# Cross-attention: row sums carried over the blocks on VectorE, and the keys' high half written by ScalarE

## What is computed

```python
def _L0_xattn_ref(hidden_states, audio_tokens, attention_mask, Wq, bq, Wk, bk, ...):
    q = proj(hs, Wq, bq, S)          # 16 heads of 32, 256 queries
    k = proj(at, Wk, bk, T)          # 4096 keys
    v = proj(at, Wv, bv, T)
    scores = einsum('bhsd,bhtd->bhst', q, k) / scale
    scores = clip(where(attend, scores, -10000.0), -50.0, 50.0)
    probs = softmax(scores, axis=-1)
    ctx = einsum('bhst,bhtd->bhsd', probs, v)
    delta = ctx @ Wo.T + bo          # then a layer norm
```

## Time and profile before

| | before |
|---|---|
| median of 3 runs | 757.49 us (756.22 to 758.24) |
| the profiled execution | 755.26 us |
| its span, first to last instruction | 753.4 us |
| PE busy | 726.6 us (96%) |
| DVE busy | 600.6 us (80%) |
| ACT busy | 413.7 us (55%) |
| PE clock granted | 1.0 of full speed over the whole span |
| the pairs of blocks 0 to 6 | 37.5 to about 301 us |
| the last block, and the rest of the cross-attention | to about 336 us |

### The profile page before, as it was taken

How to read it: one execution, slowest core, us unless ns; L and a number is a source line. 1 busy time by engine, 2 the same in 40 slices (tenths; PEclk the granted TensorE clock), 3 DMA queues, 4 the chain that set the end, 5 groups by cost and what they waited for, 6 DMA issues and landing times.

```text
span 753.4 us, 16700 instructions
## 1 busy us (share of the span) xinstructions
PE 726.6 (96%) x6859; PEld 451.1 (60%) x6859; DVE 600.6 (80%) x948; ACT 413.7 (55%) x553; POOL 10.3 (1%) x30
## 2 busy tenths in 40 slices
PE   7999999999999999898799988999999999999997
PEld 3544444444444444445677756677777777777774
DVE  4588888888888888678888975788888888888885
ACT  3567676767676767733577753444444444444441
POOL 2000000000000000001000000000000000000000
PEclk9999999999999999999999999999999999999999
DMA  8910101010100010004124320396777777777760
GB/s 318 333 61 1 58 2 58 1 58 2 58 2 2 2 58 2 2 14 200 43 105 147 135 92 1 111 291 231 232 237 239 236 231 235 232 235 242 238 209 29
DMA packets 29576, 93.79 MB, mean 124 GB/s; under 512 B 5920, under 2 KB 15056, under 8 KB 28112
## 3 DMA queue, kind: packets, MB, share of 16 engines
q1 hardware_dynamic: 29232, 92.97, 37.6%
q10 hardware_dynamic: 288, 0.02, 0.0%
HBM read 92.37 MB, written 0.57 MB: 123 GB/s over the span
## 4 chain that ended last, share of the span: by engine, by line
PE 85%; DVE 6%; issue 4%; ACT 3%; POOL 1%; POOLq 0%; DVEq 0%; ACTq 0%
PE pS L1113 38%; PE pP L1113 26%; PE pO L1113 10%; PE pD L1113 9%; DVE xT L806 2%; ACT arena L485 2%; PE pO L1441 1%; DVE arena L691 0%; DVE bn L842 0%; DVE arena L821 0%; DVE arena L941 0%; DVE arena L893 0%; DVE xn L685 0%; ACT arena L535 0%; DVE work L847 0%
## 5 line engine op out<-in xcount | busy, mean ns | idle before, releaser
L1113 PE MATMUL pS<-arena 128*128 128x256 f16 (+2 forms) x2128 | 251.5, 274 | 5.1 <-DVE arena L941 1.3
L1113 PEld LDWEIGHTS pS<-arena 128*128 128x128 f16 (+2 forms) x2128 | 210.9, 101 | 49.5 <-ACT arena L552 2.2
L1113 PE MATMUL pP<-arena 128*128 128x512 f16 x968 | 235.2, 381 | 3.2 <-DVE arena L691 3.2
L1113 PEld LDWEIGHTS pP<-arena 128*128 128x128 f16 x968 | 90.7, 98 | 127.5 <-issue 22.0
L485 ACT ACTIVATE arena<-pS,mblk 128x1024 f32<-128x1024 f32 x128 | 147.3, 1201 | 14.2 <-PE pS L1113 11.5
L941 DVE SCALAR_TENSOR_TENSOR arena<-arena 128x1536 f16<-128x1536 f32 x72 | 126.0, 1751 | 0.1
L794 DVE TENSOR_SCALAR arena<-arena 128x1024 f32<-128x1024 f32 x128 | 88.3, 692 | 45.0 <-ACT arena L485 41.8
L628 ACT ACTIVATE arena<-pS 128x256 f32<-128x256 f32 x72 | 27.6, 384 | 156.6 <-PE pS L1113 156.6
L590 ACT ACTIVATE arena<-arena 128x1536 f16<-128x1536 f32 x72 | 106.3, 1477 | 0.3 <-DMA arena<-in_units 0.3
L1113 PE MATMUL pO<-arena 128*32 128x256 f32 (+6 forms) x1358 | 103.4, 358 | 2.4 <-DVE arena L931 1.9
L1113 PE MATMUL pD<-arena 128*128 128x512 f16 x288 | 76.5, 379 | 1.0 <-DVE arena L1085 1.0
(11 more groups left out here) (232 smaller groups left out, 499.4 us busy)
## 6 DMA issues: line engine op xcount, KB each, us to landing
arena<-in_units SPq DMA_DIRECT2D x72, 768.0 KB, 4.9
arena<-w_scratch SPq DMA_DIRECT2D x136, 64.0 KB, 2.7
arena<-in_ctxT SPq DMA_DIRECT2D x7, 1024.0 KB, 5.0
mw_in<-in_mla_in SPq DMA_DIRECT2D x8, 832.0 KB, 6.0
mw_out<-in_mla_out SPq DMA_DIRECT2D x8, 512.0 KB, 3.6
wlatT<-in_wlatT SPq DMA_DIRECT2D x1, 1280.0 KB, 11.9
arena<-in_wkT SPq DMA_DIRECT2D x4, 256.0 KB, 4.7
arena<-in_ctxT SPq DMA_DIRECT2D x4, 256.0 KB, 5.8
```

The source lines that it names most:

```text
L1113: return pe.matmul(o, lhsT, rhs, start=start, stop=stop, **kw)
```

## The change

`psums` becomes four accumulators, one for each head group: the two of before, and the tiles `xn` and `x1_sb`, which have no other use in these blocks. A group is `fresh` in block 0 alone (its first add is tile 0 + tile 1: 3 adds); in blocks 1 to 6 every tile is added to the accumulator that the block before left (4 adds: two in the even pair, two in the odd). `flushed` is true in block 6 (`NBLK - 2`) alone: only then does PE call `add_sums`, once for each group. The last block is as before. Semaphore counts are computed by `adds_until` and `flushes_until`. Besides, `kh` is written by a second ACT activation from the projection's PSUM bank, ahead of that into `kf`, and DVE's copy and its wait go; DVE keeps the subtraction.

```diff
+def flushed(b, g):
+    return b == NBLK - 2
+def fresh(b, g):
+    return b == 0 or flushed(b - 1, g)
+def adds_until(b, g, tile):
+    before = sum(3 if fresh(i, j) else 4 for i in range(NBLK - 1) for j in range(HC) if (i, j) < (b, g))
+    return before + (max(1, tile) if fresh(b, g) else tile + 1)
+def flushes_until(b, g):
+    return sum(flushed(i, j) for i in range(NBLK - 1) for j in range(HC) if (i, j) <= (b, g))
...
-        psums = (psum4, xT[:, :, :])
+        psums = (psum4, xT[:, :, :], xn[:, :, :].rearrange("p t (h q) -> p (t h) q", h=2),
+                 x1_sb[:, :, :].rearrange("p t (h q) -> p (t h) q", h=2))
...
                         act.wait_ge(s["k_lo"], 4 * b + n - 1)
+                    act.activation(kh[:, p, n], bank, ACT.Identity, bias=xb[:, 1, n:n + 1], scale=1.0 / SW)
                     act.activation(kf[:, n % 2], bank, ACT.Identity, bias=xb[:, 1, n:n + 1],
...
-                            act.wait_ge(s["sum_done"], 12 * b + 3 * (g - 1) + max(1, tile))
+                            act.wait_ge(s["sum_done"], adds_until(b, g - 1, tile) if g else adds_until(b - 1, HC - 1, tile))
...
                 dve.wait_ge(s["proj_evac"], 8 * b + n + 1)
-                dve.tensor_copy(kh[:, p, n], kf[:, n % 2]).then_inc(s["k_hi"], 1)
-                dve.wait_ge(s["k_hi"], 4 * b + n + 1)
                 dve.tensor_tensor(kl[:, p, n], kf[:, n % 2], kh[:, p, n], ALU.subtract).then_inc(s["k_lo"], 1)
...
-                        acc = psums[g % 2]
-                        if tile == 0:
+                        acc = psums[g]
+                        if tile == 0 and fresh(b, g):
                             dve.wait_ge(s["clip_done"], STEPS * b + 2 * i + 2)
-                            if not (first and g < 2):
-                                dve.wait_ge(s["dsum_done"], HC * b + g - 1)
+                            if not first:
+                                dve.wait_ge(s["dsum_done"], flushes_until(b - 1, g))
                             dve.tensor_tensor(acc, probs[:, 0], probs[:, 1], ALU.add).then_inc(s["sum_done"], 1)
                         else:
-                            for t in (2, 3):
+                            for t in (tile, tile + 1):
                                 dve.wait_ge(s["clip_done"], STEPS * b + CT * g + t + 1)
-                                dve.wait_ge(s["sum_done"], 12 * b + 3 * g + t - 1)
+                                dve.wait_ge(s["sum_done"], adds_until(b, g, t) - 1)
                                 dve.tensor_tensor(acc, acc, probs[:, t], ALU.add).then_inc(s["sum_done"], 1)
...
-                pe.wait_ge(s["sum_done"], 12 * b + 3 * g + 3)
+                pe.wait_ge(s["sum_done"], adds_until(b, g, CT - 1))
...
-                    if i == 1 and not first:
+                    if i == 1 and not first and flushed(b - 1, HC - 1):
                         add_sums(b - 1, HC - 1)
-                    if i % 2 and i > 1 and not last:
+                    if i % 2 and i > 1 and not last and flushed(b, i // 2 - 1):
                         add_sums(b, i // 2 - 1)
```

More of the change, by code:

```diff
@@ L219, in build @@
             zero_ready const_ready zc_ready prep_ready wk_hi wk_lo q_mm q_f q_hi q_lo
-            ctx_hi ctx_lo proj_done proj_evac k_hi k_lo
+            ctx_hi ctx_lo proj_done proj_evac k_lo
             scores_done exp_done clip_done pv_done sum_done dsum_done
@@ L1222, in add_sums @@
             def add_sums(b, g):
-                pe.wait_ge(s["sum_done"], 12 * b + 3 * g + 3)
+                pe.wait_ge(s["sum_done"], adds_until(b, g, CT - 1))
                 for j in range(4):
-                    last = mm(pD[32 * j:32 * j + 32, 0:T], onecol[:, g, :], psums[g % 2][:, j, :], False, False,
+                    last = mm(pD[32 * j:32 * j + 32, 0:T], onecol[:, g, :], psums[g][:, j, :], False, False,
                               skip_group_check=True)
```

## The result

| | before | changed |
|---|---|---|
| median | 757.56 us (4 runs, 756.22 to 758.24) | 750.0 us (4 runs, 747.18 to 750.56) |
| ratio to before, 95% interval | | 0.9895 (0.9867 to 0.9923) |
| the profiled execution, its span | 755.26, 753.4 us | 750.56, 748.7 us |
| mean PE clock granted in it | 1.000 | 0.995 |
| PE, DVE, ACT busy | 726.6, 600.6, 413.7 us | 719.0, 610.7, 428.7 us |

The change makes the kernel 7.6 us faster by the medians; 7.8 was forecast. The page of the changed kernel has this chain, whose shares by engine are those of before; only a look at one block shows what happened.

What follows compares the result with a forecast made beforehand. PE was taken to set the pace within a block, DVE's chain at its end. 18 calls x 0.43 = 7.8 us, taken from 757.5, gave 749.7 us; range 746.3 to 754.8.

Steps and rivals of the forecast that it cites:

- 18 calls of 24 count: Of 24 removed `add_sums` calls on PE, 18 save 0.43 us each, 7.8 us in all.
- the stretch: Distance from the first scores of block 0 to those of block 7; the forecast saving was 7.8 us.
- The six calls of pair 7: `add_sums` calls in pair 7 of blocks 0 to 5: removal brings nothing, PE waits 0.82 us instead of 0.39.
- the chain: Block's end, from pair 7's scores over DVE's clips, adds and low half to PE's next projection: stays 7.04 us.
- all 24 calls count: Rival, 5%: the calls in pair 7 save time too, 10.3 us in all, giving 747.2 us.
- DVE's margin: In each pair DVE needs 4.28 us against PE's 4.46, so it has 0.18 us to spare.
- S+: Time in us after the start of PE's scores in the pair concerned.
- its lateness: DVE's second clip, 0.4 us late in pair 4, regains 0.18 a pair and is on time in pair 7.
- The first rival: Rival, 15%: DVE has no margin, a pair takes 4.52 us, five block ends come later; 4.1 saved, 753.4 us.
- the slower rival: Rival, 7%: ACT's second pass, at 1.38 us, delays PE's projection 28 times; kernel 5.4 us slower, 762.9.
- The prelude: Before the blocks, ACT's four more passes, 2.4 us, taken to cost 0 (bounds 0 and +1.1), covered by PE's query projection.
- This distance: Median of the runs, 757.49, lies 2.2 us above the profiled execution, 755.26; taken to stay.

Runs made afterwards that it cites:

- e3: Changed kernel with DVE making the context's last low half before the two adds in pair 7, not after; 744.45 us, ratio 0.9849.
- e4: Kernel before the change, with the last low half made before the adds of pair 7; 755.1 us against 756.77, ratio 0.9976.
- e1: Changed kernel with the keys' float16 copy put back on DVE, so the carried sums alone; 750.93 us, ratio 0.9932.
- e5: Changed kernel with three tiny DVE operations more in every pair of blocks 0 to 6, results unused; 751.85 us, ratio 0.9939.
- e8: Changed kernel with six tiny DVE operations more in every pair of blocks 0 to 6, results unused; 760.86 us, ratio 1.0052.
- e2: Kernel before the change with ACT's second pass alone, writing the keys' high half, sums as before; 757.35 us, ratio 1.0011.

## Why the prediction was right

*18 calls of 24 count.* Shown. Forecast for the stretch 7.8, measured 7.77. The six calls of pair 7 came back as six longer waits for the low half (0.42 each, 0.43 forecast; a wait is 0.73 us on average and was 0.32, where the prediction had 0.82 and 0.39 from starts), the chain kept its 7.03, and e3 turned the waits into time as soon as the chain was shortened. The rival "all 24 calls count" was the right size (10.4 by e3 and e4) for another kernel, one in which DVE's order at the block's end is changed too.

*DVE's margin.* Shown, and as narrow as read: 4.27 us a pair by e1, 4.28 forecast. In the changed kernel itself the low halves of pairs 4, 5 and 6 of block 3 are 4.27 and 4.28 apart, and the second clip starts at S+3.41 in pair 5 and S+3.22 in pairs 6 and 7, so DVE has made up its lateness as it was forecast (S+3.43, S+3.25 and S+3.22):

```profile
171.59 0.69 DVE L714 SCALAR_TENSOR_TENSOR arena<-arena 128x512 f16<-128x512 f32 x1
172.19 1.29 DVE L815 TENSOR_SCALAR arena<-arena 128x1024 f32<-128x1024 f32 x2
...
175.86 0.69 DVE L714 SCALAR_TENSOR_TENSOR arena<-arena 128x512 f16<-128x512 f32 x1
...
180.14 0.69 DVE L714 SCALAR_TENSOR_TENSOR arena<-arena 128x512 f16<-128x512 f32 x1
```

The first rival, each instruction at its whole duration, would have given 4.52 and a chain that is 0.74 longer; it did not happen. Its mechanism, a DVE without margin that makes the block's end late, is real, though: e5 and e8 take the margin away, PE is held up at the blocks' ends and nowhere else, and with six operations more the whole gain of the change is gone. By the Trainium skill, "VectorE: DVE Perf Modes", § The DRAIN you can't avoid, the next operation waits for the pipe to empty, but a "next op that is not held starts earlier". The prediction weighed the first half alone; the trace, with 0.06 us start to start for operations 0.14 long, goes with the second.

*Busy time was forecast too high.* DVE's grew by 10.1 us and not 17.5, ACT's by 15.0 and not 22. The forecast added up durations; busy time counts overlapping ones once, and what was added runs back to back. A block shows it: 34.06 busy, which is 8 x 4.27 = 34.2 and not the 35.2 of the sum. For the same reason 96% load was too dark a figure: it was 93%. The time itself was worked out from starts and is not touched. PE's busy time fell by 7.6 us and not by about 10. In the stretch it did fall by 10.4, from 261.66 to 251.30; behind the stretch it is 3.3 us longer, where PE has the lower clock in two places. The stretch before and after:

```profile
37.48:300.99 263.51, 261.66 (x3116) 121.07 (x3115) 221.40 (x277) 178.78 (x195) 0.00 (x0) 1.00 0.08 26
```

```profile
37.87:293.61 255.74, 251.30 (x2925) 114.77 (x2925) 232.88 (x273) 191.73 (x223) 0.00 (x0) 1.00 0.08 27
```

*ACT.* Shown: 0.58 start to start (0.59 forecast), exps at S+1.26 (1.28), and the slower rival, a pass of 1.38, is far off. e2 shows that the pass costs nothing where it stands.

*The prelude.* The first scores come at 37.87 instead of 37.48. The 0.4 us are there before any key is evacuated: ACT's last conversion of a context chunk, which waits for its load, starts at 10.97 and not 10.58, and the first evacuation at 20.17 and not 19.78. The queries' evacuation, behind all four passes, starts at 27.61 and not 27.23, so nothing is added. And in e2, which has the same four passes, the first scores are at 37.62. Over the ten kernels of this study the first scores lie between 36.95 and 37.87. So the passes themselves were hidden, as taken.

*Before the change the median lies 2.2 us above the profiled execution.* This distance was taken to stay, without a reason. It did not: the profiled execution of the changed kernel was forecast at 747.5 us and took 750.56, 0.6 above its median. That the median came out near its forecast all the same was luck: most executions of both kernels have a lower clock, which the prediction did not know. The 2.2 are the lower clock after PE's waits in the self-attention: the profiled execution of before had none of it, three of the four executions of the changed kernel had it (mean clock 0.993 to 0.995, 749.9 to 750.6 us), the fourth had the full clock and took 747.18. Compared at the same clock, the change is worth 755.4 - 747.2 = 8.2 us at full clock (one execution) and about 757.5 - 750.2 = 7.3 at 0.993 to 0.995.

## What to carry to other kernels

Count a removed instruction only where its engine sets the pace: follow the chain of waits through each stage, and where another engine's chain is the longer one there, what is removed comes back as a wait; then shorten that chain as well, here by moving one operation of DVE ahead of two. To tell whether an engine has room, take the start-to-start times of a stretch in which it waits for nobody, not its durations and not its busy share. Where executions differ in their clock, a stretch between two fixed points of the trace tells more than a median.

## What the runs showed of the hardware

PE's granted clock fell to 0.50, 1.2 GHz, for some 3 us after series of waits none of which was longer than 1.9 us, in about two of three executions of one and the same kernel, at a cost of 1.4 to 2.1 us on average; after a single wait of 2.5 us it fell in two places of one execution of e8 and not in three others. 27 matmuls of zeros in the waits of the first kind took nearly all of it away and made ten executions agree within 1.1 us. Why the clock falls behind the same waits in one execution and not in another stays open. Where it waits for nothing, DVE starts an instruction before the one ahead of it has ended: 0.60 us start to start for 0.69 long clips, 0.06 for 0.14 long operations on one element. Where it has to wait for the one ahead, as the second add of a pair does, it is 1.33 from start to start for 1.22 long ones (two in 2.55).
